# A graph layer's message pass: source rows taken from a table of products instead of from x

## The reference

```python
def _mlp(x, W1, b1, W2, b2):
    return relu(x @ W1 + b1) @ W2 + b2
msg_in = concatenate([nodes[row], nodes[col], edge_features], axis=-1)   # 64 + 64 + 32
messages = _mlp(msg_in, mW1, mb1, mW2, mb2)                              # 160 -> 128 -> 64
aggregated = segment_sum(messages, col, num_segments=12500)
upd_in = concatenate([nodes, aggregated], axis=-1)
out = layernorm(x + _mlp(upd_in, uW1, ub1, uW2, ub2))                    # row = src, col = dst
```

## Time and profile before

| | |
|---|---|
| timed runs | 1991.9 us (1990.66 to 1992.25) |
| profiled execution, its span | 2629.5 us (the profile gives no other time of it) |
| PE, matmuls | 2171.8 us busy, 83% |
| PE, weight loads | 1907.7 us busy, 73% |
| POOL | 1500.2 us busy, 57% |
| DVE, ACT | 785.5 us and 787.3 us busy, 30% each |
| clock granted to TensorE, mean | 0.78 of full speed |
| DMA | 89.82 MB, 34 GB/s |

### The profile page before, as it was taken

The page is one execution under the profiler, slowest core; times in us unless marked ns, Lnnn a source line. Parts: engine busy times, 40 slices in busy tenths (PEclk is TensorE's granted clock), DMA queues, the critical chain, the costliest instruction groups (busy, mean ns, idle before and its releaser), DMA issues.

```text
span 2629.5 us, 44108 instructions
## 1 busy us (share of the span) xinstructions
PE 2171.8 (83%) x14372; PEld 1907.7 (73%) x14372; DVE 785.5 (30%) x2197; ACT 787.3 (30%) x2078; POOL 1500.2 (57%) x1572
## 2 busy tenths in 40 slices
PE   2988888888888788888888888888888888888897
PEld 2877777777768677777787767777677767777676
DVE  3222222222222222222222333333333333333334
ACT  3222222222222222222223333333333333333333
POOL 6655555555556555665555555555555555555550
PEclk9777677777776867787777788877877877787878
DMA  5111111111111111111111111111111111111110
GB/s 118 36 34 32 32 34 32 32 32 32 33 32 33 34 31 32 32 35 32 32 30 31 32 33 32 32 31 33 32 31 31 33 32 32 31 31 34 31 32 19
DMA packets 97107, 89.82 MB, mean 34 GB/s; under 512 B 58534, under 2 KB 58954, under 8 KB 96730
## 3 DMA queue, kind: packets, MB, share of 16 engines
q0 software_dynamic: 50016, 51.32, 11.0%
q1 hardware_dynamic: 33610, 30.90, 4.5%
q10 hardware_dynamic: 13458, 7.31, 1.3%
HBM read 86.20 MB, written 3.21 MB: 34 GB/s over the span
## 4 chain that ended last, share of the span: by engine, by line
PE 56%; another core or an unknown queue 20%; issue 14%; DVE 5%; ACT 3%; ACTq 1%; DVEq 1%; DMA 0%; SPq 0%
PE bank L280 13%; PE bank L281 13%; PE bank L291 11%; PE bank L266 5%; PE bank L256 5%; PE bank L295 3%; PE bank L253 3%; DVE oh_t L343 1%; PE bank L638 1%; PE bank L631 1%; ACT xe L310 1%; PE bank L625 1%; ACTq L364 1%; DVE xc L360 1%
## 5 line engine op out<-in xcount | busy, mean ns | idle before, releaser
L234 POOL DMA_INDIRECT xg<-x_rows,slot_idx x1563 | 1499.1, 959 | 1071.1 <-DVE slot_idx L349 636.9
L280 PE MATMUL bank<-w_xe,xe 97*128 97x128 f32 x3128 | 792.5, 340 | 58.7 <-issue 57.4
L281 PE MATMUL bank<-win_tab,oh_t 96*128 96x128 f32 x3128 | 768.0, 332 | 69.0 <-issue 67.7
L281 PEld LDWEIGHTS bank<-win_tab,oh_t 96*128 96x128 f32 x3128 | 622.7, 244 | 79.7 <-issue 78.8
L280 PEld LDWEIGHTS bank<-w_xe,xe 97*128 97x128 f32 x3128 | 620.9, 244 | 75.8 <-issue 75.3
L333 DVE TENSOR_TENSOR oh<-iota,rel 128x384 f32<-128x384 f32 x391 | 218.3, 559 | 1306.5 <-remote 980.0
L291 PE MATMUL bank<-oh,hid 128*128 128x96 f32 x3128 | 535.6, 321 | 55.6 <-issue 53.8
L310 ACT ACTIVATE xe<-bank 64x256 f32<-64x256 f32 x782 | 295.7, 378 | 897.2 <-remote 580.3
L291 PEld LDWEIGHTS bank<-oh,hid 128*128 128x128 f32 x3128 | 505.3, 241 | 74.2 <-issue 72.7
L325 ACT ACTIVATE hid<-bank 128x512 f32<-128x512 f32 x391 | 230.8, 590 | 785.2 <-remote 440.8
L343 DVE COPY oh_t<-bank 96x512 f32<-96x512 f32 x391 | 268.5, 687 | 474.7 <-remote 294.6
(11 more groups left out here) (58 smaller groups left out, 533.2 us busy)
## 6 DMA issues: line engine op xcount, KB each, us to landing
xe<-edge_t SPq DMA_DIRECT2D x391, 64.0 KB
xg<-x_rows,slot_idx POOLq DMA_INDIRECT x1563
xc<-x_t ACTq DMA_DIRECT2D x4, 800.0 KB
resid<-x_rows SPq DMA_DIRECT2D x24, 128.0 KB
out<-resid ACTq DMA_DIRECT2D x24, 128.0 KB
resid<-dst_groups SPq DMA_DIRECT2D x1, 784.0 KB
dst_i<-dst_tiles ACTq DMA_DIRECT2D x1, 784.0 KB
src_idx<-src_all SPq DMA_DIRECT2D x1, 784.0 KB
```

The costliest lines, as they stand in the source:

```text
L234: pool.indirect_dma_start(out=xg[:, k, j * D:(j + 1) * D], out_offset=None, in_=x_rows, in_offset=bass.IndirectOffsetOnAxis(ap=slot_idx[:, ...
L280: nc.tensor.matmul(o, xe[:, r, j * P:(j + 1) * P], w_xe[:, :], start=True, stop=False)
L281: last = nc.tensor.matmul(o, oh_t[:, q, j * P:(j + 1) * P], win_tab[:, r, :], start=False, stop=True)
```

## The change

Two tables are made in DRAM before the loop, each 12544 rows of 128: `src_table` is x by the first part of mW1, `dst_table` is x by the second part plus mb1. In the loop:
- `gather` fetches rows of `src_table` (512 bytes) into `ag`; they are not transposed.
- `load_window`, new, brings the window's 96 rows of `dst_table` by a DMA of SP into `picked`, whose partitions 96 to 127 hold the edge part of mW1. `picks` has the turned one-hot in partitions 0 to 95 and the edge features in 96 to 127.
- `hidden` adds the gathered rows by one f32 product of 512 columns whose weights are the identity, and has one product of 128 columns per tile (`picks` by `picked`) in place of two.
- `transpose_x`, `copy_x` and `pick_window` are gone; the one-hot copy moves from DVE to ACT, and has two PSUM banks. `next_indices` waits for `hidden` of its own group.
- POOL waits for the whole `src_table` before its first gather; SP and ACT wait for the whole `dst_table` before the loop.

```diff
-                    out=xg[:, k, j * D:(j + 1) * D], out_offset=None, in_=x_rows,
+                    out=ag[:, k, j * DH:(j + 1) * DH], out_offset=None, in_=src_table,
...
+        def load_window(sp, g, k, base):
+            r = k % RING
+            wait(sp, s_h, g - RING + 1)
+            sp.dma_start(picked[0:WIN, r, :], dst_table[ds(base, WIN), :]).then_inc(s_window[r], 16)
...
         def hidden(pe, g, k, lap):
             q, r = k % 2, k % RING
             n = lap * (UNROLL // RING) + k // RING + 1
-            wait(pe, s_xe, g + 1)
-            wait(pe, s_edge[r], n * 16)
             wait(pe, s_oht, g + 1)
+            wait(pe, s_edge[r], n * 16)
+            wait(pe, s_window[r], n * 16)
             wait(pe, s_relu, g - 1)
+            missing = G_END * TPG - T_END if isinstance(g, int) and g == G_END - 1 else 0
+            wait(pe, s_gathered[k], (lap + 1) * 16 * TPG - 16 * missing)
+            nc.tensor.matmul(ps_h[q][:, :], ident[:, :], ag[:, k, :], start=True, stop=False)
             for j in range(TPG):
-                o = ps_h[q][:, j * DH:(j + 1) * DH]
-                nc.tensor.matmul(o, xe[:, r, j * P:(j + 1) * P], w_xe[:, :], start=True, stop=False)
-                last = nc.tensor.matmul(o, oh_t[:, q, j * P:(j + 1) * P], win_tab[:, r, :],
-                                        start=False, stop=True)
+                last = nc.tensor.matmul(ps_h[q][:, j * DH:(j + 1) * DH], picks[:, r, j * P:(j + 1) * P],
+                                        picked[:, r, :], start=False, stop=(j == TPG - 1))
             last.then_inc(s_h, 1)
...
+        def copy_oh(g, k):
+            act = nc.scalar
+            q, r = k % 2, k % RING
+            wait(act, s_oht_mm, g + 1)
+            wait(act, s_h, g - RING + 1)
+            act.activation(picks[0:WIN, r, :], ps_o[q][0:WIN, :], ACT.Copy).then_inc(s_oht, 1)
...
         def next_indices(g, k):
             dve = nc.vector
-            wait(dve, s_xt_mm, g + 1)
+            wait(dve, s_h, g + 1)
...
+        def pe_table(s_mm, s_cp, w):
+            pe = nc.tensor
+            for n in range(TSTEPS):
+                wait(pe, s_cp, n - 3)
+                for b in range(step_blocks(n)):
+                    at = (n * TB + b) * P
+                    if w is w_src:
+                        pe.wait_ge(s_xt[at * 4 // NODES], 16)
+                        pe.wait_ge(s_xt[(at + P - 1) * 4 // NODES], 16)
+                    last = nc.tensor.matmul(banks[n % 4][:, b * DH:(b + 1) * DH], xc[0:D, at:at + P],
+                                            w[:, :], start=True, stop=True)
+                last.then_inc(s_mm, 1)
+        def store_src_table(sp, steps):
+            for n in steps:
+                sp.wait_ge(s_a_cp, n + 1)
+                sp.dma_start(table_rows(src_table, n),
+                             a_out[n % ASLOTS][:, 0:step_blocks(n) * DH].rearrange("p (b n) -> p b n", n=DH)
+                             ).then_inc(s_a_st[n % ASLOTS], 16)
...
             pool.wait_ge(s_first, 16)
+            src_table_stored(pool)
             for k in range(UNROLL):
                 gather(pool, k, k)
...
+            store_src_table(sp, range(0, 4))
             sp.wait_ge(s_win, 5)
             for to, of in ((base_f_dram, base_f), (spread_dram, spread), (lag_dram, lag), (base_i_dram, base_i)):
                 sp.dma_start(to.rearrange("(p g) -> p g", g=GPP), of[:, :]).then_inc(s_scratch, 16)
+            store_src_table(sp, range(4, 10))
             sp.wait_ge(s_scratch, 64)
...
+            store_src_table(sp, range(10, TSTEPS))
             sp.dma_start(src_idx[:, 0:TILES], src_all).then_inc(s_src, 16)
+            store_dst_table(sp)
...
+            pe.wait_ge(s_wsrc, 16)
+            pe_table(s_a_mm, s_a_cp, w_src)
+            pe.wait_ge(s_wdst, 16)
+            pe.wait_ge(s_a_cp, TSTEPS)
+            pe_table(s_b_mm, s_b_cp, w_dst)
```

More of the change, by code:

```diff
@@ L143, in build @@
         base_all = resid[:, 2 * GPP * GE:2 * GPP * GE + GROUPS]
[L145 to L146 removed]
+        a_out = [ag[:, n, :] for n in range(ASLOTS)]
+        b_out = [picks[:, n, :] for n in range(RING)] + [hid[:, n, :] for n in range(BSLOTS - RING)]
         upd_h = [dst_i[:, v * CN:(v + 1) * CN].bitcast(f32) for v in range(TAIL)]
@@ L187, in build @@
         s_opened = sem("s_opened")
-        s_picked = sem("s_picked")
-        s_xt_mm = sem("s_xt_mm")
-        s_xe = sem("s_xe")
+        s_window = [sem(f"s_window{i}") for i in range(RING)]
         s_oh = sem("s_oh")
@@ L366, in window_bases, with stored_steps, src_table_stored, dst_table_stored @@
                 skip_runtime_bounds_check_because="the chip clamps them to this range")[1]
-        def table_stored(eng):
-            for n in range(TSLOTS):
-                eng.wait_ge(s_tab_st[n], TSTEPS // TSLOTS * 16)
+        def stored_steps(n, slots):
+            return len(range(n, TSTEPS, slots))
+        def src_table_stored(eng):
+            for n in range(ASLOTS):
+                eng.wait_ge(s_a_st[n], stored_steps(n, ASLOTS) * 16)
+        def dst_table_stored(eng):
+            for n in range(BSLOTS):
+                eng.wait_ge(s_b_st[n], stored_steps(n, BSLOTS) * 16)
@@ new lines, in act_src_table, with dve_dst_table @@
+        def act_src_table():
+            act = nc.scalar
+            for n in range(TSTEPS):
+                w = step_blocks(n) * DH
+                act.wait_ge(s_a_mm, n + 1)
+                wait(act, s_a_st[n % ASLOTS], n // ASLOTS * 16)
+                act.activation(a_out[n % ASLOTS][:, 0:w], banks[n % 4][:, 0:w], ACT.Copy).then_inc(s_a_cp, 1)
+        def dve_dst_table():
+            dve = nc.vector
+            dve.wait_ge(s_b1, 16)
+            for n in range(TSTEPS):
+                nb = step_blocks(n)
+                dve.wait_ge(s_b_mm, n + 1)
+                wait(dve, s_b_st[n % BSLOTS], n // BSLOTS * 16)
+                dve.tensor_tensor(b_out[n % BSLOTS][:, 0:nb * DH].rearrange("p (b n) -> p b n", n=DH),
+                                  banks[n % 4][:, 0:nb * DH].rearrange("p (b n) -> p b n", n=DH),
+                                  b1_rows[:, None, :].to_broadcast([P, nb, DH]), ALU.add).then_inc(s_b_cp, 1)
@@ L848, in windowed @@
             def windowed():
-                act.wait_ge(s_xt, 64)
-                for g, base in zip(range(2), window_bases(ET.Activation, 0, 2)):
-                    pick_window(g, g, base)
-                copy_x(0, 0)
+                dst_table_stored(act)
+                copy_oh(0, 0)
                 def lap(i, c):
-                    first = i * UNROLL + 2
-                    bases = window_bases(ET.Activation, first, min(UNROLL, G_END - first) if
-                                         isinstance(i, int) else UNROLL)
                     for k in range(UNROLL):
```

201 lines of the change are left out of this document (78 added, 123 removed).

## The result

| | before | after |
|---|---|---|
| timed runs | 1991.99 us (1990.66 to 1992.25, 4 runs) | 2064.59 us (2062.64 to 2066.54, 4 runs) |
| ratio, 95% interval | | 1.0369 [1.0354, 1.0384] |
| profiled execution, its span | 2629.5 us | 2064.7 us |
| granted clock, mean | 0.78 | 0.93 |

The change costs 72.6 us, 3.7%. I had forecast 39 us and a range that ends at 2056. The profiled execution of the changed kernel took 2066.5 us, as long as the timed runs, so this profile is of the runs that it must explain; that of before, of an execution 638 us longer than its timed runs, was not.

A forecast was written before the change was run, and what follows sets the result against it. The prediction took POOL's stream of gathers to bound the timed runs, with PE waiting. 33rd gather at 96, plus 1937 for the rest as before, less 2 for PE's tail, gave 2031 us, 2.0% slower; range 2012 to 2056.

The forecast's parts named there:

- The lighter PE: Loop: PE loses 0.7 us a group, worth nothing while gathers come every 5.00 us.
- Rival A: Loop: PE bounds the timed runs at mixed clocks and gathers are quicker unprofiled; about 1750 us; chance 0.12.
- Rival B: Gathers: POOL's time follows the row's bytes; 3478 us at double time, 2184 for 0.1 us more; chance 0.06.
- Rival C: Loop: PE, with less to do, idles and stays at half clock, 6.05 us a group; 2487 us; chance 0.04.
- Rival D: Whole kernel: the lighter PE removes as much as the start costs; 1985 to 2000 us, about no change; chance 0.05.
- It is stored between 83 and 98, I take 88: Start: when the destination table is stored, in us; its 25 PE steps begin about 49 and need 23 to 43 us.
- Before, it went at 54.8: Start of the kernel before: the 33rd gather taken to go at 54.8 us, leaving 1937 us of the 1991.9.
- First gather: Start: POOL's first gather waits for the source table's 25 stores; 53 us, 46 to 58 as ends.
- 33rd gather 109.6 against 96: Start: the 33rd gather waits for group 0's hidden and the destination table; forecast at 96 us, range 90 to 108.
- the 2 us of PE tail: End of the kernel: a shorter PE tail, 2 us subtracted from the sum.
- the agreement of 1987 with 1992: Kernel before: POOL's floor, 3.5 + 1954 + 29 = 1987 us, against 1991.9 measured, taken to show that gathers bind.
- I expect the profile to get much shorter although the timed runs get longer: Profiled execution: start adds 41 us, loop shrinks from 6.4 to 5.1 to 5.4 us a group; span 2120 to 2260.

The follow-up runs named there:

- e10: The changed kernel without both tables, gathers (512-byte rows) and windows reading the edge features: 2484.59 us, ratio 0.9448 to the kernel before.
- e11: The changed kernel without both tables, gathers fetching 256-byte rows of x instead of 512-byte rows: 2482.81 us, ratio 0.946 to the kernel before.
- e2: The kernel before with only the first two of the four gathers of each group: 1653.73 us, ratio 0.621 to the kernel before.
- e3: The changed kernel with only the first two of the four gathers of each group: 1532.15 us, ratio 0.5749 to the kernel before.
- e5: The changed kernel, unchanged, measured again: 2060.48 us, ratio 1.0350 to the kernel before.
- e8: The changed kernel with table products over 128 rows of contraction instead of 64, the added weights zero: 2044.77 us, ratio 1.0271 to the kernel before.
- e13: The changed kernel, unchanged, where the kernel before takes 2620 to 2670 us: 2605.7 us, ratio 0.9767 to the kernel before.
- e18: The kernel before with the one-hot made by four tensor_scalar comparisons instead of one tensor_tensor; three such runs took 2654.23 to 2704.34 us, ratios 1.0111 to 1.0135.

## Why the prediction was wrong in size and right in kind

**Right, and shown.** The timed runs are bound by POOL. For the changed kernel its trace shows it. For the kernel before, of which there is no trace in that condition, it follows from a sum: in each of the 20 traces the median gather takes 0.944 to 0.947 us with 0.305 to the next, and 3.5 + 1562 x 1.249 + 21 (the tail of after) = 1975 us, an estimate of the least that it can take, leaves 17 us of the 1992. Bytes per row don't enter (959 ns in both, and e10 beside e11). The lighter PE is worth nothing in that condition: it saves 0.47 us a group on its own account (e2 against e3), and all of it turns into waiting for gathers. Of the 72.6 us of loss 62.9 lie ahead of the 33rd gather; 9.7 don't. Rival A (PE bounds the timed runs) is false for these; that PE bounds holds in the long condition. Rival B fell with 959 ns. Rival C fell: PE was idle a quarter of the time at a mean clock of 0.93. The Trainium skill, page "TensorE: Matmul & The Clock Gate", section "Why this matters for your kernels", warns that idle gaps put the clock back to half; the trace agrees that it dips, and not that it stays down. The rival had a grain of truth: in the set of e5 to e8 the clock is 0.99 in the kernel before and 0.93 to 0.94 in the changed one (e5), whose PE has less to do. Rival D fell with the 3.7%.

**Wrong: the size of the start.** The step that failed is the second table's, "It is stored between 83 and 98, I take 88", together with the base it was compared with, "Before, it went at 54.8". I had the start add 41 us and it added 62.9. The terms are these.

- First gather: 53 forecast, 58.4 measured. The prediction's sum with PE at half clock throughout (9 + 43 + 1 + 3 = 56) had the right terms, and I chose 3 us below it; I had in mind, a fully busy half-clock stretch of 13 us that is followed by full clock. Those were products of 96 to 128 rows but for the window's; the tables' 64-row products never left half clock in 86 us. The rest is x_t, whose first quarter let PE begin at 11.3, not 9: +5.4.
- Second table: it begins at 55.05 where I had 49, takes 43.0 us, all at half clock, and has landed at 101.2 (ACT's row above), past even the upper end of my 83 to 98: +13.2 against the 88. From there to the 33rd gather it is 8.4 us against 8 (windows from 101.95, the first group at half clock from 104.46): +0.4. 33rd gather 109.6 against 96: +13.6. With tables mostly at full clock (e8) it goes at 90.7, ahead of my 96, so the clock that I took is what made the term too small.
- The base. "Before, it went at 54.8" is wrong: that row is the 37th gather. Counted out, the 32nd and the 33rd of the kernel before stand here on POOL's timeline, with only the 0.30 us between them:

```profile
45.41 0.94 POOL L234 DMA_INDIRECT xg<-x_rows,slot_idx  x1 [0.30 <-issue]
46.66 0.94 POOL L234 DMA_INDIRECT xg<-x_rows,slot_idx  x1 [0.30 <-issue]
```

  The shift is 109.6 - 46.7 = 62.9 us, where I subtracted unlike things and got 41: +8.1 from this alone.
- From the 33rd gather to the end: 2064.59 - 109.6 = 1955.0 against 1991.99 - 46.7 = 1945.3, +9.7 (and the 2 us of PE tail that I took off did not come). The cause of this part stays open; 46.7 is from a trace of the long condition. 1530 periods from 109.59 to 2043.64 are 1.264 us each, 0.944 + 0.305 and 0.015 of long gathers; I had used 1.25 from two rows at the end while the mean of 959 ns already said 1.264. By it the old floor is 3.5 + 1563 x 1.264 + 21 (the tail of after, 2064.7 - 2043.6) = 2000, *above* the 1992 measured. So the agreement of 1987 with 1992 that carried my argument was in part luck: a period too short by 0.014 us (22 us in all) against a tail taken 8 us too long and a loop that was in fact quicker than 1.264. In the short condition the kernel before must have fewer long gathers than the 23.6 us of after (by the sum above at most some 17), or a shorter tail. That would account for most of the 9.7, but I have no trace of it there.

13.6 + 8.1 + 9.7 + 2 = 33.4 us, the 33.6 between 2031 and 2064.59.

**Right for the wrong reason.** "I expect the profile to get much shorter although the timed runs get longer" came true because the second profile was taken in the short condition. In the long one the changed kernel's span is 2604.0 (e13), not 2120 to 2260: a lighter PE does not shrink the holes in proportion. After the 33rd gather PE has 230 idle stretches of 0.5 us and more that the profile gives to "issue" in the first trace of the kernel before, 210 us in sum, and 303 in e13, 397 us in sum. And the holes are the smaller part of what makes that condition long: the same 14372 matmul records keep PE busy for 2171.8 us in the kernel before and for 1585.9 in e2, at a clock of 0.78 and 0.996. The prediction, which spoke of PE's holes alone, missed these 586 us.

## What to carry to other kernels

Find the first instruction of the bounding engine that the change can delay (here the 33rd gather) by counting, and take its start before and after: the difference is most of the loss (here 62.9 of 72.6 us), since everything behind a saturated queue follows it one to one. While one engine is saturated, work taken from another is worth nothing, and a setup phase that delays the saturated one is paid in full. Price a burst by a row of the same contraction and type at either clock; being busy is no promise of the full clock. And when the profiled execution and the timed runs disagree by a third, as here, take both kernels again before using either: here the sign depended on it.

## What the runs showed of the hardware that I had not expected

- **Contraction and clock.** f32 products with 64 rows of contraction, back to back for 43.0 us twice with 0.78 us between, ran at half clock to the end (1.72 us for four); the same with 128 rows took 1.06 us for four in their first 12.76 us, so the clock rose within that stretch, after 3.8 us of it (e8).
- **Two conditions.** One kernel, 1990.65 us in one set and 2625.57 to 2668.33 in others, with a clock of 0.99 and of 0.77 to 0.79, and in the long ones with holes of 0.5 to 2.2 us between matmuls that the profile gives to "issue". Instruction fetch moved 0.3 MB in all in either condition (after, e13), and the gathers' packets of the changed kernel took 127 ns on average in the short one and 117 in the long one (q0's 19.2% and 14.0% of 16 engines' span over 50016 packets), so neither explains them. With half of the gathers, in such a set, the kernel before has no such hole (e2) and the changed kernel 15 (e3), so they go with the full stream of gathers beside PE. Their cause is open, and so is what belongs to the chip and what to the time: each set was one chip.
- **A comparison on DVE lengthens gathers on POOL**, up to 1.33 us for 0.94, in sum 23.0 us of 1499. The Trainium skill, page "SBUF — State Buffer", section "Who interferes with whom", says that a DVE instruction with two SBUF inputs contends with a GpSimd instruction that reads SBUF, and that one with at most one SBUF input, outside of DVE's two-port modes, does not. The traces agree in both halves: the 186 gathers that begin beside an addition of one PSUM and one SBUF input in after take 0.03 us more in sum, and with one tensor input (e18) the excess is 0.7 us. The pair of rows that shows it, POOL's and DVE's timelines of after:

```profile
2030.90 1.20 POOL L222 DMA_INDIRECT ag<-src_table,slot_idx  x1 [0.30 <-issue]
2032.41 0.94 POOL L222 DMA_INDIRECT ag<-src_table,slot_idx  x1 [0.30 <-issue]
```

```profile
2030.72 0.56 DVE L302 TENSOR_TENSOR oh<-iota,rel 128x384 f32<-128x384 f32 x1 [2.20 <-PE bank L276]
```
